# A linear-attention and mixture-of-experts kernel: three expert-weight buffers, earlier slot opening, a halved first chunk

## The reference

```python
xn = layernorm(x)
q, k, v = split(xn @ W_qkv); k = layernorm_noaffine(k)        # per head of 8
# causal linear attention: intra-chunk scores, masked, plus a running state S
scores = where(causal, einsum('bthd,bshd->bhts', q_c, k_c), 0)
y = einsum('bhde,bthe->bthd', S, q_c) + einsum('bhts,bshd->bthd', scores, v_c)
S = S + einsum('bthd,bthe->bhde', v_c, k_c)
attn = y @ W_o
# routed experts on xn, top 1 of 8
aff = xn @ centroids.T; assign = argmax(aff, 1); a = sigmoid(aff)
h = relu((layernorm(xn) * ln_g + ln_b) @ w1.T + b1); ye = xn + h @ w2.T + b2
ffn = a * ye + (1 - a) * xn          # of the assigned expert
out = x + attn + ffn
```

## Time and profile before

| | us |
|---|---|
| median of 3 runs | 501.4 |
| lowest, highest | 495.81, 501.7 |
| profiled execution | 499.43 |
| its span, first to last instruction | 497.6 |
| mean granted TensorE clock, share of full speed | 0.951 |
| busy: PE, DVE, ACT, POOL | 425.5, 313.2, 266.9, 262.6 |

### The profile page before, as it was taken

How to read it: one execution, slowest core, us unless ns; L and a number is a source line. 1 busy time by engine, 2 the same in 40 slices (tenths; PEclk the granted TensorE clock), 3 DMA queues, 4 the chain that set the end, 5 groups by cost and what they waited for, 6 DMA issues and landing times.

```text
span 497.6 us, 13064 instructions
## 1 busy us (share of the span) xinstructions
PE 425.5 (86%) x4571; PEld 313.5 (63%) x4572; DVE 313.2 (63%) x836; ACT 266.9 (54%) x692; POOL 262.6 (53%) x279
## 2 busy tenths in 40 slices
PE   1889999999999688795978696858999999999993
PEld 1455656565656455462645453438889999999892
DVE  3678897897966986664764556434555656656551
ACT  4678767776765564341424142104666666666661
POOL 5033333333233243674766464732777778777765
PEclk9999999999999998999989797967999999999998
DMA  7993133121100111403041313121445454444530
GB/s 236 272 247 96 33 87 86 27 62 43 45 28 16 44 40 48 129 29 119 29 124 39 103 39 107 60 76 23 65 56 69 64 72 63 66 65 66 66 49 0
DMA packets 63454, 37.21 MB, mean 75 GB/s; under 512 B 5480, under 2 KB 61088, under 8 KB 63392
## 3 DMA queue, kind: packets, MB, share of 16 engines
q1 hardware_dynamic: 50976, 27.86, 21.5%
q0 software_dynamic: 12416, 8.54, 12.2%
HBM read 18.79 MB, written 18.10 MB: 74 GB/s over the span
## 4 chain that ended last, share of the span: by engine, by line
PE 63%; DVE 11%; DMA 9%; issue 8%; ACT 3%; SPq 1%; another core or an unknown queue 1%; POOL 1%; ACTq 1%; POOLq 1%; DVEq 0%
PE bank L942 12%; PE bank L973 11%; PE bank L1056 10%; PE bank L1064 9%; DMA w2raw<-in_L_ffn_w_dram 4%; DVE pr L621 4%; PE bank L888 3%; PE bank L981 3%; PE bank L929 3%; PE bank L893 3%; PE bank L960 2%; DMA out_dram<-qx,xs 2%; DMA xs<-slots_d 2%; PE bank L1049 1%; DVE res L635 1%
## 5 line engine op out<-in xcount | busy, mean ns | idle before, releaser
L308 POOL TENSOR_SCALAR_AFFINE_SELECT pr<-pr 128x512 f32<-128x512 f32 x104 | 65.3, 646 | 161.1 <-ACT pr L417 160.3
L354 POOL DMA_INDIRECT out_dram<-qx,xs x72 | 111.9, 1554 | 52.5 <-DVE qx L814 30.0
L621 DVE TENSOR_TENSOR pr<-bank,causal 128x512 f32<-128x512 f32 x152 | 96.6, 683 | 32.7 <-PE bank L942 28.2
L509 ACT ACTIVATE qx<-bank,b1T 128x128 f32<-128x128 f32 x288 | 82.6, 368 | 57.0 <-PE bank L1056 55.1
L973 PEld LDWEIGHTS bank<-pr,vz 128*32 128x32 f32 x2048 | 56.5, 114 | 62.6 <-issue 61.1
L417 ACT ACTIVATE pr<-bank 128x512 f32<-128x512 f32 x104 | 57.8, 598 | 63.4 <-PE bank L942 45.3
L942 PE MATMUL bank<-qx,kT 32*128 32x512 f32 x512 | 80.5, 682 | 11.0 <-DVE pr L621 11.0
L1056 PE MATMUL bank<-qx 128*128 128x128 f32 x576 | 78.7, 281 | 7.8 <-issue 3.5
L973 PE MATMUL bank<-pr,vz 128*32 128x128 f32 x2048 | 79.3, 288 | 5.4 <-issue 5.2
L1056 PEld LDWEIGHTS bank<-qx 128*128 128x128 f32 x576 | 71.7, 196 | 9.6 <-issue 5.9
L1064 PE MATMUL bank<-xT,qx 128*128 x576 | 77.0, 277 | 0.5 <-ACT qx L509 0.5
(11 more groups left out here) (129 smaller groups left out, 497.7 us busy)
## 6 DMA issues: line engine op xcount, KB each, us to landing
slots_d<-zrow SPq DMA_DIRECT2D x8, 594.0 KB, 9.8
xs<-slots_d SPq DMA_DIRECT2D x72, 66.0 KB
xin<-in_L_attn_x_dram SPq DMA_DIRECT2D x8, 512.0 KB, 4.4
res<-in_L_attn_x_dram SPq DMA_DIRECT2D x16, 256.0 KB, 3.6
out_dram<-res SPq DMA_DIRECT2D x16, 256.0 KB
w1raw<-in_L_ffn_w_dram SPq DMA_DIRECT2D x8, 256.0 KB
w2raw<-in_L_ffn_w_dram SPq DMA_DIRECT2D x8, 256.0 KB
out_dram<-qx,xs POOLq DMA_INDIRECT x72
```

Source lines behind the costliest of these rows:

```text
L308: pool.affine_select(out=pv, in_=pv, compare_op=ALU.is_ge, fill=0.0, base=0, pattern=[[0, J], [1, P]], channel_multiplier=-1).then_inc(s(" ...
L354: pool.indirect_dma_start(out_rows, bass.IndirectOffsetOnAxis(ap=xs[:, a, D + 2:D + 3].bitcast(U32), axis=0), ye[:, a, :], None, bounds_ch ...
L509: last = nc.scalar.activation(ht[:, k % 2, c * P:(c + 1) * P], SC[2 + k % 2][:, c * P:(c + 1) * P], ACT.Relu, bias=b1T[:, bass.ds(e * FC + ...
L621: nc.vector.tensor_tensor(pr[:, m % 2, g, :].rearrange("p (j t) -> p j t", j=J), SC[g][:, :].rearrange("p (j t) -> p j t", j=J), bcast(cau ...
```

## The change

- Weights in RAW = 3 buffers, experts 0 to 2 loaded at the start, the next one (n-6) as SP opens step n, ahead of the store.
- ROUTED 38 instead of 40, three scatters after every tile's mask from there.
- w1s, xss and xsT get memory of their own. In tile 62 the DVE loads the expert registers, copies w1 of slot 0 and scales slots 0 and 1; TensorE transposes them before the last products and multiplies slot 0 before the last output projection; ACT copies their transposes before the last y.
- Chunk 0 is loaded and normalised in halves (steps 0 and 1, two tiles by ACT and two by the DVE each); k is projected first, v into a bank of its own; q_copy has a semaphore of its own, and ACT copies the second half's transpose after the root of k.

```diff
-    BY_ACT = 6
-    ROUTED = 40
+    ROUTED = 38
+    STEPS = [(0, 0, B // 2), (0, B // 2, B)] + [(c, 0, B) for c in range(1, NCH)]
+    RAW = 3
-        w1raw = sb("w1raw", [P, 2, FC, D])
-        w2raw = sb("w2raw", [P, 2, F])
+        w1raw = sb("w1raw", [P, RAW, FC, D])
+        w2raw = sb("w2raw", [P, RAW, F])
+        w1s = sb("w1s", [P, 2, F])
+        xss = sb("xss", [P, 2, D])
+        xsT = sb("xsT", [P, 2, D])
...
             def load_expert(e):
-                reach(sp, s("w1_ps"), e - 1)
-                reach(sp, s("w2_ps"), e - 1)
-                reach(sp, s("b1_fold"), e - 1)
+                reach(sp, s("w1_ps"), e - RAW + 1)
+                reach(sp, s("w2_ps"), e - RAW + 1)
+                reach(sp, s("b1_fold"), e - RAW + 1)
...
-            load_tokens(0)
+            for st, (c, lo, hi) in enumerate(STEPS[:2]):
+                sp.dma_start(xin[:, c, lo:hi, :], x_v[:, c, lo:hi, :]).then_inc(s(f"x_in{st}"), 16)
...
+                if n >= 9 and n - 9 + RAW < E:
+                    load_expert(n - 9 + RAW)
                 if n:
                     store_quad(n - 1)
-                if n >= 9 and n - 7 < E:
-                    load_expert(n - 7)
-                if n:
                     load_resid(n + 1)
...
                 if m >= ROUTED:
-                    for _ in range(3 if m % 3 else 2):
+                    for _ in range(3):
...
# ACT, start
-            ln_norm(0, range(4))
-            ln_norm(0, range(4, BY_ACT))
+            ln_root(1)
+            ln_norm(0, (0, 1))
+            ln_norm(1, (4, 5))
             xT_copy(0, SC[0])
...
+            k_square(0)
             q_copy(0)
-            xT_copy(1, SC[1])
-            k_square(0)
             k_root(0)
+            xT_copy(1, Y[0])
...
# ACT, end
-            y_copy(NQ - 1)
+            se_xT(0)
+            se_xT(1)
+            y_copy(NQ - 1)
             act.wait_ge(s("b1_fold"), E)
             act.wait_ge(s("eid_ready"), 1)
             regs = expert_registers(act)
-            se_xT(0)
-            se_xT(1)
...
# DVE, start
             ln_stats(0)
+            ln_stats(1)
+            ln_norm(0, (2, 3))
...
+            ln_norm(1, (6, 7))
...
# DVE, tile 62, behind its masks
+                if m == NT - 2:
+                    dve.wait_ge(s("w1_sb"), E)
+                    dve.wait_ge(s("eid_ready"), 1)
+                    regs = expert_registers(dve)
+                    e = load_experts(dve, regs, 0)
+                    se_weights(0, e[2])
+                    se_scale(0)
+                    se_scale(1)
             result(NQ - 1)
...
# TensorE, start
-            q_project(0)
             kT_project(0)
-            x_transpose(1, SC[1])
+            q_project(0)
+            v_project(0, Y[1])
+            x_transpose(1, Y[0])
             k_transpose(0)
-            v_project(0)
-            pe.wait_ge(s("xT_sb"), 2)
...
# TensorE, end
-            products(NT - 1)
-            output(NQ - 1)
-            pe.wait_ge(s("w2_sb"), E)
             pe.wait_ge(s("se_sb"), act_before(NT))
             pe.wait_ge(s("so_sb"), dve_before(NT))
+            se_trans(0)
+            se_trans(1)
+            products(NT - 1)
+            se_up(0)
+            output(NQ - 1)
+            pe.wait_ge(s("w2_sb"), E)
             pe.wait_ge(s("eid_ready"), 1)
             regs = expert_registers(pe)
-            se_trans(0)
-            se_trans(1)
```

More of the change, by code:

```diff
@@ L238, in _ @@
                 zero_slots(i)
-            load_expert(0)
-            load_expert(1)
+            for e in range(RAW):
+                load_expert(e)
             def store_quad(n):
@@ L363, in _, with ln_root, ln_norm @@
         def _(act):
[L364 to L367, removed]
+            def ln_root(st):
+                c, lo, hi = STEPS[st]
+                act.wait_ge(s("mv_ready"), st + 1)
+                if c >= 2:
+                    act.wait_ge(s("rstd_ready"), c)
+                nc.scalar.activation(std[:, c % 2, lo:hi], mv[:, c * B + lo:c * B + hi, 1], ACT.Sqrt, bias=eps[:, 0:1])\
                     .then_inc(s("std_ready"), 1)
-            def ln_norm(c, tiles):
-                act.wait_ge(s("nmr_ready"), c + 1)
+            def ln_norm(st, tiles):
+                c = STEPS[st][0]
+                act.wait_ge(s("nmr_ready"), st + 1)
                 for b in tiles:
@@ L733, in experts_of_slots @@
                     .then_inc(s("eid_ready"), 1)
[L735 to L789, removed]
             def se_scale(k):
@@ L816, in se_result @@
                                                op1=ALU.add).then_inc(s("ye_ready"), 1)
+            kT_copy(0)
+            kn_copy(0)
+            k_var(0)
+            k_rstd(0)
+            dve.wait_ge(s("vz_zero"), 2 * HALF)
+            v_scale(0, Y[1])
+            for m in range(NT):
+                n, i = m // HALF, m % HALF
+                more = n + 1 < NQ
+                for g in by_dve(m):
+                    score_mask(m, g)
+                if i == 0:
+                    if n + 1 < NCH:
+                        ln_stats(n + 2)
+                    if more:
+                        kT_copy(n + 1)
+                    if n == 8:
+                        choose(3)
+                    if n == 9:
+                        places()
+                if i == 1:
+                    if n + 1 < NCH:
+                        ln_norm(n + 2, (6, 7))
+                    if more:
+                        kn_copy(n + 1)
+                    if n:
+                        result(n - 1)
+                    if n in (2, 4, 6):
+                        choose(n // 2 - 1)
+                    if n == 8:
+                        count(3)
+                        second_norm()
+                    if n == 9:
+                        experts_of_slots()
+                if i == 2:
+                    if more:
+                        k_var(n + 1)
+                        k_rstd(n + 1)
+                        v_scale(n + 1, FA)
+                    if n == 8:
+                        tiles_of_experts()
+                if i == 3:
+                    if n < NQ - 2:
+                        dstate_mask(n)
+                    if n < 8 and n % 2 == 1:
+                        aff_copy(n // 2)
+                    if n in (2, 4, 6):
+                        count(n // 2 - 1)
+                    if n == 8:
+                        second_rstd()
+                    if n >= 8 and n - 8 < E:
+                        if n == 8:
+                            dve.wait_ge(s("lb_in"), 16)
+                        b1_fold(n - 8)
+                if m == NT - 2:
[6 more added lines that the diff above has]
+                    se_scale(1)
@@ L819, in _ @@
+            result(NQ - 1)
             dve.wait_ge(s("sc_ps"), NT)
             dve.wait_ge(s("b2_in"), 16)
[L821 to L828, removed]
             se_scale(2)
@@ L917, in w2_transpose @@
                 for c in range(FC):
-                    last = nc.tensor.transpose(FA[:, c * P:(c + 1) * P], w2raw[:, e % 2, c * P:(c + 1) * P], ident[:, :])
+                    last = nc.tensor.transpose(FA[:, c * P:(c + 1) * P], w2raw[:, e % RAW, c * P:(c + 1) * P], ident[:, :])
                 last.then_inc(s("w2_ps"), 1)
@@ L1079, in _ @@
                     k = RING * i + a
-                    se_up(k)
+                    if k:
+                        se_up(k)
                     if k + 2 < NS:
```

99 lines of the change are left out of this document (53 added, 46 removed).

## The result

| | before | after |
|---|---|---|
| median of 4 runs, us | 498.61 | 474.54 |
| lowest, highest | 495.48, 501.7 | 471.09, 477.48 |
| profiled execution, its span | 499.43, 497.6 | 471.09, 469.3 |
| mean granted clock | 0.951 | 0.982 |

The median before is of four executions here, of three in the table further up. The ratio is 0.9515, 95% interval 0.9411 to 0.9618: faster, by about 24 us. The forecast was 464 in a range of 453 to 479, so the time lies in the range, 10.5 above the value named. In the profiled executions the span fell by 28.3 us where 36.3 were forecast. The profiled execution after is the fastest of its four. Where some executions of the kernel before were slow ones, over 1.5% above its fastest, the ratios of the experiments leave them out, so they can differ a little from the medians.

The account below looks back on a forecast made before the run. TensorE's gaps and slow clock bound it, mainly weight waits; GpSimd binds next. Span 497.6 less 36 (25.5 quads plus 12.6 bridge, 2 given back) less 0.3 start is 461.3; execution 463.1, forecast 464; own range 458 to 470, with rivals 453 to 479.

Parts of the forecast that it names:

- Weights: Six quads, 175.50 to 311.54 us: three buffers and earlier loads end all six `w1_transpose` waits, 20.8 us.
- GpSimd's queue as the next bound: Quads 10 to 14: masks, scatters and `state_add` take GpSimd 18.9 us a quad, above TensorE's 16.5; 25.5 us gained.
- a sign of being wrong: Wrong if quads stay above 20, the clock stays at 0.90, or the expert part is no longer 152.
- drips hide under GpSimd's pace: Six quads: single matmul groups with 0.3 us issue gaps, some 8 us, hidden by slack of about 4 us.
- rival 1: Quads: drips add on top beside denser scatters; up to 8 us come back, 472 us. Chance 0.22.
- the bridge: Last quad to first expert output scatter: 21 us instead of 33.6, gain 12.6; 2 given back for drips.
- Start: First chunk loaded and normalised in halves: first projection about 10.5 instead of 11.47, gain 0.3 us, bounds -1 and +1.5.
- rival 2: Quads: the DVE's third-tile chain or the transposed-weight copy sets about 20.5 us a quad; about 483 us. Chance 0.08.
- rival 3: Quads: GpSimd doesn't bind, TensorE's 16.5 decides, 10 us less; 454 us with the bridge at full speed. Chance 0.12.
- rival 4: Quads: idle under GpSimd's pace keeps TensorE at 1.2 GHz, 28 to 30 us a quad; near 525 us. Chance 0.03.

Follow-up runs that it names:

- e9: The changed kernel itself, run again in the third set beside a new run of the kernel before: 474.91 us, ratio to before 0.9523.
- e8: The changed kernel without the early opening of the first expert slots, put back behind the last output: 465.36 us, ratio to before 0.9596.
- e3: The changed kernel with no token scatter in the attention loop, all 64 sent behind it: 534.56 us, one execution.
- e12: The changed kernel with the DVE masking all four score groups from tile 38 on, GpSimd and ACT none: 513.06 us, one execution.
- e10: As e12, but GpSimd waits for a tile's scores before that tile's three scatters: 469.74 us, ratio to before 0.9422.

## Why the prediction was right, and where it was off

**Weights.** Right. All six waits ended, and nothing queued on SP behind the earlier load came late. The part is worth 17.2 us beside e9's 24.5.

**GpSimd's queue as the next bound.** In the changed kernel's own profile this didn't come true: no wait of TensorE for GpSimd, quads 10 to 14 at 19.6 to 21.6 instead of 18.9, the clock of the stretch at 0.94 instead of above 0.95. Four of the five quads are above 20, which the prediction itself had named as a sign of being wrong. In e8, in a set without late stretches, mechanism and size were right: 18.7 us a quad, TensorE waiting before the products as named.

**The step that failed** is "drips hide under GpSimd's pace". I had put them at 8 us over six quads and hidden by 4 us of slack. They are late stretches of 3.8 to 5.3 us; the one in quad 12 costs TensorE 4.78 us, all that the quad takes above its 16.0. GpSimd waits 1.68 us for the score copy in it, so that its 18.9 us of work and this wait fill the same 20.6: its queue is nearly full, but TensorE doesn't wait for it. The six quads so gave 13.5 us instead of 25.5.

This is rival 1, given a chance of 0.22. e3 shows that without scatters there are no late stretches; beside e12's unbroken runs they are longest. "Scatters fill the DMA engines" doesn't hold, by the 13.4% above, and that TensorE waits for its own instructions is not shown: in that window the DMA queues that carry instructions moved nothing.

The Trainium skill (DMA: Bandwidth & Descriptors, "Issuing engines are not separate DMA queues") tells that all transfers share 16 engines. That doesn't explain the late stretches: the engines were busy for 13.4% in one, and e12 and e10 send the same scatters per quad over the same engines and differ by 8.5 us of the DVE's idle time.

**Luck in the number.** That the span came out 8.0 us above the forecast 461.3, the price of rival 1, is partly chance: the six quads fell short by 12.0, while the bridge was 3.3 better than reckoned with its drips and the expert part 1.0. The median lies another 2.5 above what I had added for it. At 474.5 the time is outside my own 458 to 470 and inside the wide range only through its rivals. As a ratio the forecast was 0.925 (464 over 501.4), and no set reached it: 0.9515 and 0.9523 with late stretches, and an estimated 0.95 without them (e8's 465.4 less the 5.5 to 6.9 of the bridge, over 483.7).

**The bridge.** 21 us forecast plus 2 for drips, 19.7 measured: the 2 weren't needed. The register load came out shorter than its row: the DVE stood idle for 1.12 us ahead of the copy of w1 in tile 62. The slots had landed by then. The Trainium skill's price (Runtime: NRT & Kernel Launch, "Instruction fetch mechanics") would give an estimated 2.2 for eleven registers. It stands there for loads from HBM, this kernel loads them from on-chip memory, and the 1.12 here and the 1.55 of the earlier trace rows decide.

**Start.** 0.3 forecast; the `q_project` at 154.57 starts at 154.44, 0.13 won. First k projection at 10.56, forecast 10.5. This part wasn't run alone, nor was the scatter rate.

**The other rivals.** The DVE's chain didn't take the stall's place (rival 2): e3's 16.0 excludes it. But its price was mis-added: quads of 20.5 with the bridge as forecast give 471.7 of span and about 474 us, not 483, and that is the time that was measured, by another cause. GpSimd does bind once late stretches are away (e8, against rival 3). The clock was 0.94 over the six quads and didn't stay low (against rival 4).

**What stays open.** What holds TensorE's signals and matmuls back beside a run of scatters, and why a whole set of runs is free of it, wasn't found. No run separates GpSimd's own work on a scatter from its transfer, and the changed kernel was never run in a set free of late stretches.

## What to carry to other kernels

Before removing a stall, look for the engine that catches up during it: here GpSimd's queue, whose cost of one mask and three scatters a tile gave the length of a quad to within 0.2 us in e8, where nothing else came in between. Small "issue" gaps beside another engine's DMAs are worth a trial of their own before they are called hidden; leave the DMAs out once and look. And where GpSimd sends many indirect DMAs in a row beside dense matmuls, try breaking them up: a wait that held them back in threes made 28 us quads 20 us ones here. Run a kernel and what it is compared with in one set; 15.7 us lay between two sets of the same kernel.

## What the runs showed of the hardware that I had not expected

- Beside indirect DMAs of GpSimd, with the DMA engines busy for only 13.4%, TensorE slowed down and its results reached the DVE and ACT late. The DVE idled up to 11.2 us beside twelve in a row (8.3 of it behind the end of the matmul; e12), 2.5 to 5.3 us beside groups of three with a mask between (the changed kernel and e9), 2.7 beside groups of three held back by the scores (e10). Without them in the loop there was none of it (e3, in a set that otherwise had it).
- The same chip and the same kernel gave 483.7 us in one set of runs and 499.4 in another; the traces of other kernels in the first set were free of these stretches, those of the second had them.
- A scatter of one tile took GpSimd 0.97 us and a gap of 0.30, so one mask and three scatters came every 4.38 us (e8).
